# The end of a sixteen-head attention: its last twenty units over six PSUM banks, and a split output projection

## The reference

```python
keys    = xn @ triu(Wk).T        # xn: layer-normalised x
queries = xn @ tril(Wq).T
values  = xn @ Wv.T              # each reshaped to (b, t, 16, 8)
att = softmax(queries . keys * scale)
x = x + (att . values).reshape(b, t, 128) @ Wu.T + bu
```

## Time and profile before

| | |
|---|---|
| median of 3 runs | 1685.22 us (1685.16 to 1686.24) |
| the profiled execution's own time | 1684.64 us |
| its span | 1682.9 us |
| mean granted clock of TensorE | 0.951 of full speed |
| PE busy | 1525.1 us (91%) |
| DVE busy | 1378.1 us (82%) |
| ACT busy | 921.6 us (55%) |
| POOL busy | 300.4 us (18%) |

### The profile page before, as it was taken

How to read it: one execution, slowest core, us unless ns; L and a number is a source line. 1 busy time by engine, 2 the same in 40 slices (tenths; PEclk the granted TensorE clock), 3 DMA queues, 4 the chain that set the end, 5 groups by cost and what they waited for, 6 DMA issues and landing times. The chain is left out here.

```text
span 1682.9 us, 24089 instructions
## 1 busy us (share of the span) xinstructions
PE 1525.1 (91%) x8530; PEld 759.5 (45%) x8530; DVE 1378.1 (82%) x2435; ACT 921.6 (55%) x1751; POOL 300.4 (18%) x366
## 2 busy tenths in 40 slices
PE   6899999999999999869998888876999969989698
PEld 2111111111111111158884333332788758869587
DVE  6999999999999997357673999999766657887686
ACT  3088888888888888823334666663422232222232
POOL 3200000000000000000012888785000110020000
PEclk7599999999999999979999999999999988999799
DMA  3340011000000000200000212221000002200123
GB/s 96 108 146 24 26 30 31 28 24 23 23 23 24 24 24 5 51 9 1 1 1 24 78 65 68 70 67 34 1 1 1 1 1 97 80 28 1 51 75 104
DMA packets 41233, 66.07 MB, mean 39 GB/s; under 512 B 11422, under 2 KB 18511, under 8 KB 40392
## 3 DMA queue, kind: packets, MB, share of 16 engines
q1 hardware_dynamic: 41112, 64.52, 12.7%
HBM read 56.72 MB, written 6.88 MB: 38 GB/s over the span
## 5 line engine op out<-in xcount | busy, mean ns | idle before, releaser
L785 DVE TENSOR_REDUCE row_max<-ps 128x1 f32<-128x1024 f32 x512 | 601.0, 1219 | 34.3 <-PE ps L590 18.1
L708 ACT ACTIVATE probs<-ps 128x512 f32<-128x512 f32 x1024 | 529.0, 604 | 127.6 <-PE ps L605 127.3
L605 PE MATMUL ps<-q_stack,k_stack 51*128 51x512 bf16 x1024 | 346.9, 387 | 8.7 <-ACT probs L708 6.7
L590 PE MATMUL ps<-k_stack,q_stack 48*128 48x512 bf16 x1024 | 325.9, 404 | 20.3 <-DVE row_max L785 10.6
L622 PE MATMUL ps<-probs,v_head 128*16 128x512 f32 x2048 | 270.0, 600 | 0.0
L590 PEld LDWEIGHTS ps<-k_stack,q_stack 48*128 48x128 bf16 x1024 | 58.7, 96 | 368.3 <-DVE row_max L785 342.0
L1298 PE MATMUL ps<-s_hc,ident 128*128 128x512 f32 x256 | 139.0, 628 | 47.8 <-DVE s_hc L1571 42.8
L951 ACT ACTIVATE x_gate<-ps 128x512 f32<-128x512 f32 x128 | 76.3, 598 | 183.8 <-PE ps L122 183.6
L1223 POOL TENSOR_TENSOR s_dbx<-s_dx,s_b_rows 128x512 f32<-128x512 f32 x128 | 159.4, 1270 | 35.1 <-DVE s_h L1562 34.6
L1562 DVE TENSOR_TENSOR_SCAN s_h<-ps,s_state,s_dbx 128x512 f32<-128x512 f32 x128 | 156.7, 1264 | 4.6 <-POOL s_dbx L1223 2.8
L605 PEld LDWEIGHTS ps<-q_stack,k_stack 51*128 51x128 bf16 x1024 | 76.1, 94 | 131.7 <-ACT probs L708 128.1
(11 more groups left out here) (339 smaller groups left out, 1866.9 us busy)
## 6 DMA issues: line engine op xcount, KB each, us to landing
s_b_rows<-s_b_dram SPq DMA_DIRECT2D x64, 256.0 KB, 3.1
y_spread<-y_probs_dram SPq DMA_DIRECT2D x128, 128.0 KB, 3.0
q_stack<-q_parts_dram SPq DMA_DIRECT2D x30, 96.0 KB
k_stack<-k_parts_dram SPq DMA_DIRECT2D x30, 96.0 KB
w_w<-w_dram SPq DMA_DIRECT2D x1, 2048.0 KB, 8.0
o_dram<-o_sb SPq DMA_DIRECT2D x64, 32.0 KB
q_stack<-q_parts_dram SPq DMA_DIRECT2D x30, 64.0 KB
k_stack<-k_parts_dram SPq DMA_DIRECT2D x30, 64.0 KB
```

The source lines that it names most:

```text
L590: last = nc.tensor.matmul(core.ps[:, 2 * b + r, :], qst[buf][0:KROWS, u * P:(u + 1) * P], kst[buf][0:KROWS, key:key + CH], start=True, sto ...
L605: nc.tensor.matmul(core.ps[:, S_BANK + n % S_RING, :], kst[buf][HALF:ROWS, kt * P:(kt + 1) * P], qst[buf][HALF:ROWS, c * CH:(c + 1) * CH], ...
L708: nc.scalar.activation(probs[:, us % RING, c * CH:(c + 1) * CH], core.ps[:, S_BANK + n % S_RING, :], ACT.Exp).then_inc(exp_done, 1)
L785: nc.vector.tensor_reduce(mx[:, u, b:b + 1], core.ps[:, 2 * b:2 * b + 2, :], mybir.AxisListType.XY, ALU.max).then_inc(max_done, 1)
```

## The change

- **Twenty units by themselves.** The units 236 to 255 (`TAIL` to `UNITS`), whose scores came in `slot` after the last maxima, get a loop of their own. Scores go in turn to the six banks 6, 4, 5, 0, 1, 2 and wait for the exp six places back; the first three still for the one three back; the fourth and the sixth also for the last maxima. Odd scores read rows 0 to 50 of the stacks, even ones rows 64 to 114. For that the ones and maxima of heads 14 and 15 are also placed in rows 48 to 50, by four added DMAs (two of ones at the start, one behind each head's maxima).
- **Heads 0 to 13** are loaded before head 15's maxima are stored in SP's list, and divided as before. **Head 14** goes the way that head 15 went (`late`), into rows 112 to 119 of `attT`.
- **Projection of heads 0 to 14** (rows 0 to 119 of `attT`): four groups of four matmuls, behind the values of the units 251 to 254, all into bank 3. DVE adds each to `x`, and the next group waits for that.
- **Head 15** isn't stored. PE takes `o_sb` itself as the weight, rows 32c to 32c+15, against `Wu_last`, a new weight array of 129 columns: 8 rows of Wu's last head, a ninth whose last column is 1, which brings the denominator, and zeros. The sixteen matmuls write three tiles to bank c and the fourth to bank 4+c. DVE takes the reciprocals of the denominators (two instructions per chunk) and adds each tile times its reciprocal to `x` (16 `scalar_tensor_tensor`). The next norm's statistics come after the second chunk instead of the first.
- Filling `attT` and `den` with ones at the start is dropped.

The core of the diff:

```diff
+    UNITS = HEADS * NT
+    TAIL = UNITS - LAG_S
+    TAIL_BANKS, EARLY_OUT_BANK, LAST_TILES = (6, 4, 5, 0, 1, 2), 3, 3
+    OUT_UNITS = range(UNITS - NC_ - 1, UNITS - 1)
...
@@ sync
                 sp.dma_start(qst[par][HALF + KROWS:ROWS, :], md[par]).then_inc(m_loaded[par], 16)
+                if head >= HEADS - 2:
+                    sp.dma_start(qst[par][KROWS:KROWS + NPART, :], md[par]).then_inc(low_loaded[head % 2], 16)
...
+            for head in (HEADS - 2, HEADS - 1):
+                sp.dma_start(kst[head % NBUF][KROWS:KROWS + NPART, :], ones[:]).then_inc(low_ones_placed, 16)
...
             store_o(HEADS - 3)
+            sp.wait_ge(o_stored, O_STORE * (HEADS - 2))
+            for which, dst in enumerate((attT, den)):
+                sp.dma_start(dst[0:MOST, :], od[which, 0:HEADS - 2]).then_inc(fin_loaded, 16)
             store_max(HEADS - 1, (HEADS - 1) % NBUF)
             store_o(HEADS - 2)
-
             sp.wait_ge(o_stored, O_STORE * (HEADS - 1))
-            sp.wait_ge(cleared, 2)
-            for which, dst in enumerate((attT, den)):
-                sp.dma_start(dst[0:FULL, :], od[which, 0:HEADS - 1]).then_inc(fin_loaded, 16)
-            store_o(HEADS - 1)
-            sp.wait_ge(o_stored, O_STORE * HEADS)
             for which in range(2):
                 sp.dma_start(late[:, which, :],
-                             od[which, HEADS - 1].rearrange("s (k n) -> (s k) n", n=P)).then_inc(late_loaded, 16)
-            sp.wait_ge(att_ready, NC_)
+                             od[which, HEADS - 2].rearrange("s (k n) -> (s k) n", n=P)).then_inc(late_loaded, 16)
             sp.wait_ge(late_ready, 1)
-            sp.dma_start(attT[FULL:P, :].rearrange("s (k n) -> s k n", n=P), late[:, 0, :]).then_inc(late_placed, 16)
+            sp.dma_start(attT[MOST:FULL, :].rearrange("s (k n) -> s k n", n=P), late[:, 0, :]).then_inc(late_placed, 16)
@@ tensor
+            def tail_score(n):
+                m, c = TAIL + n // NC_, n % NC_
+                head, kt = m // NT, m % NT
+                buf = head % NBUF
+                if n == 0 or kt == 0 and c == 0:
+                    pe.wait_ge(m_loaded[buf], 16 * (m // BODY + 1))
+                    pe.wait_ge(low_loaded[head % 2], 16)
+                if n in (3, 5):
+                    pe.wait_ge(max_done, 2 * UNITS - 1 + n // 5)
+                if n < S_RING:
+                    pe.wait_ge(exp_done, 4 * TAIL + n - S_RING + 1)
+                elif n >= len(TAIL_BANKS):
+                    pe.wait_ge(exp_done, 4 * TAIL + n - len(TAIL_BANKS) + 1)
+                rows = slice(0, KROWS + NPART) if n % 2 else slice(HALF, ROWS)
+                nc.tensor.matmul(core.ps[:, TAIL_BANKS[n % len(TAIL_BANKS)], :], kst[buf][rows, kt * P:(kt + 1) * P],
+                                 qst[buf][rows, c * CH:(c + 1) * CH], start=True, stop=True).then_inc(s_done, 1)
+
+            def project_out(g):
+                if g == 0:
+                    core.loaded(pe, "Wu0", "Wu_last")
+                    pe.wait_ge(att_ready, NC_)
+                    pe.wait_ge(late_placed, 16)
+                    pe.wait_ge(max_done, 2 * UNITS)
+                else:
+                    pe.wait_ge(out_added, g)
+                for k in range(TPC):
+                    last = nc.tensor.matmul(core.ps[:, EARLY_OUT_BANK, k * P:(k + 1) * P],
+                                            attT[0:FULL, (g * TPC + k) * P:(g * TPC + k + 1) * P], w["Wu0"][0:FULL, :],
+                                            start=True, stop=True)
+                last.then_inc(out_done, 1)
...
-            for gs in range(NT + LAG_V):
-                slot(LOOPED, gs, gs < NT, gs < NT + LAG_S)
-
-            core.loaded(pe, "Wu0")
-            pe.wait_ge(att_ready, NC_)
-            pe.wait_ge(late_placed, 16)
-            for g in range(NC_):
+            for gs in range(NT):
+                slot(LOOPED, gs)
+            pe.wait_ge(low_ones_placed, 32)
+            for m in range(TAIL, UNITS):
+                for c in range(NC_):
+                    tail_score(NC_ * (m - TAIL) + c)
+                weigh_values(m - 2)
+                if m in OUT_UNITS:
+                    project_out(m - OUT_UNITS.start)
+            weigh_values(UNITS - 2)
+            weigh_values(UNITS - 1)
+
+            pe.wait_ge(evacuated, HEADS)
+            pe.wait_ge(out_added, NC_)
+            for c in range(NC_):
                 for k in range(TPC):
-                    last = nc.tensor.matmul(core.ps[:, g, k * P:(k + 1) * P], tile_of(attT, g * TPC + k), w["Wu0"][:],
-                                            start=True, stop=True)
-                last.then_inc(out_done, 1)
+                    bank, col = (c, k * (P + 1)) if k < LAST_TILES else (NC_ + c, 0)
+                    last = nc.tensor.matmul(core.ps[:, bank, col:col + P + 1],
+                                            o_sb[32 * c:32 * c + VROWS, k * P:(k + 1) * P],
+                                            w["Wu_last"][32 * c:32 * c + VROWS, :], start=True, stop=True)
+                last.then_inc(last_done, 1)
@@ scalar
+            for m in range(TAIL, UNITS):
+                if m % NT == 2:
+                    evacuate(m // NT - 1)
+                act.wait_ge(pv_done, m - (RING - 1))
+                for c in range(NC_):
+                    n = NC_ * (m - TAIL) + c
+                    act.wait_ge(s_done, 4 * TAIL + n + 1)
+                    nc.scalar.activation(probs[:, m % RING, c * CH:(c + 1) * CH],
+                                         core.ps[:, TAIL_BANKS[n % len(TAIL_BANKS)], :], ACT.Exp).then_inc(exp_done, 1)
@@ vector
+                nc.vector.tensor_tensor(xs, xs, core.ps[:, EARLY_OUT_BANK, :].rearrange("p (k d) -> p k d", d=P),
+                                        ALU.add).then_inc(out_added, 1)
+            for c in range(NC_):
+                dve.wait_ge(last_done, c + 1)
+                t = c * TPC
+                outs = core.ps[:, c, 0:LAST_TILES * (P + 1)].rearrange("p (k n) -> p k n", n=P + 1)
+                nc.vector.reciprocal(last_rden[:, t:t + LAST_TILES], outs[:, :, P]).then_inc(last_rden_ready, 1)
+                nc.vector.reciprocal(last_rden[:, t + LAST_TILES:t + TPC],
+                                     core.ps[:, NC_ + c, P:P + 1]).then_inc(last_rden_ready, 1)
+                dve.wait_ge(last_rden_ready, 2 * (c + 1))
+                if c == 0:
+                    dve.wait_ge(out_added, NC_)
+                for k in range(TPC):
+                    part = outs[:, k, 0:P] if k < LAST_TILES else core.ps[:, NC_ + c, 0:P]
+                    line.mark(nc.vector.scalar_tensor_tensor(out=core.x[:, t + k, :], in0=part,
+                                                             scalar=last_rden[:, t + k:t + k + 1],
+                                                             in1=core.x[:, t + k, :], op0=ALU.mult, op1=ALU.add))
+                if c == 1:
                     line.wait(dve)
                     following.stat_rows(dve, 0)
```

More of the change, by code:

```diff
@@ L302, in softmax_attention @@
         late = sb("late", [P, 2, P])
-        FULL = (HEADS - 1) * HD
+        MOST, FULL = (HEADS - 2) * HD, (HEADS - 1) * HD
+        last_rden = sb("last_rden", [P, NT])
         qd = nc.dram_tensor("q_parts_dram", (HEADS, NPART, HD, T), BF16).ap()
@@ L346, in softmax_attention @@
         fin_loaded = core.sem("a_fin_loaded")
-        cleared = core.sem("a_cleared")
+        low_ones_placed = core.sem("a_low_ones_placed")
+        low_loaded = [core.sem(f"a_low_loaded{i}") for i in range(2)]
         late_loaded = core.sem("a_late_loaded")
@@ L354, in softmax_attention @@
         out_done = core.sem("a_out_done")
+        out_added = core.sem("a_out_added")
+        last_done = core.sem("a_last_done")
+        last_rden_ready = core.sem("a_last_rden_ready")
         bias_added = core.sem("a_bias_added")
@@ L507, in _ @@
                 stage_v(head, head)
-            for a in (attT, den):
-                nc.gpsimd.memset(a[:], 1.0).then_inc(cleared, 1)
             core.loaded(pool, "bu")
@@ L568, in _, with weigh_values @@
             core.loaded(pe, "Wv0")
+            def weigh_values(m):
+                buf, kt = m // NT % NBUF, m % NT
+                if kt == 0:
+                    pe.wait_ge(v_staged, m // NT + 1)
+                    if m:
+                        pe.wait_ge(evacuated, m // NT)
+                pe.wait_ge(exp_done, 4 * m + 4)
+                for c in range(NC_):
+                    last = nc.tensor.matmul(core.ps[32 * c:32 * c + VROWS, O_BANK, :], v_head[buf][:, kt, :],
+                                            probs[:, m % RING, c * CH:(c + 1) * CH],
+                                            start=kt == 0, stop=kt == NT - 1)
+                last.then_inc(pv_done, 1)
@@ L613, in slot @@
                 if values:
[L614 to L625, removed]
+                    weigh_values(j * BODY + gs - LAG_V)
             for gs in range(BODY):
@@ L725, in _ @@
```

(26 more changed lines are left out.)

## The result

| | before | after |
|---|---|---|
| median | 1685.73 us (4 runs, 1685.16 to 1687.53) | 1668.30 us (4 runs, 1667.05 to 1668.85) |
| profiled execution: time, span | 1684.64, 1682.9 | 1668.66, 1666.9 |

The ratio is 0.9894, 95% interval 0.9877 to 0.9911: faster, by 17.4 us or 1.1%. Forecast were 1669.5 and a range of 1666 to 1674.

A forecast was written before the change was run, and what follows sets the result against it. DVE's maxima pace the attention; the last twenty units were bound by a loop through PE, the end by one chain. Tail -7.5, exit -9.4 and clock +1.2 gave -15.7, so 1669.5 us, range 1666 to 1674.

The forecast's parts named there:

- Tail: Last twenty units to the last values' end: six banks let ACT pace, -9.1 us; -7.5 us together with the added projections.
- Projections: Four groups for the other heads amid the last units, 1.1 us of PE each, 2.63 per unit: +2.2 us.
- Inputs: Loads and placed rows for the last units arrive in time: cost 0, or 0.5 us if head 15's load lands late.
- Head 14's margin: Time between head 14's placing and the first projection's need of it, at unit 251: 6.3 us.
- Rival D: Early projection's inputs late, stopping PE in unit 251; beyond 6.3 us each microsecond costs one, 5 would give 1674.5; chance 0.05.
- Rival B: Paired scores in the last units don't run side by side; 2.4 us more, 1672; chance 0.08.
- Rival C: ACT doesn't keep 0.485 with more banks, or the loop closes elsewhere; only the exit gains, 1677; chance 0.05.
- rival E: PE's clock falls in the last twenty units because it is less busy there; 1694; chance 0.03.
- Exit: From the last values to the norm rows' end: 10.1 us against 19.55, DVE pacing at 1.39 per chunk; -9.4 us.
- Clock: PE stands about 5 us while DVE finishes, so the next stage runs longer at half clock; +1.2 us, bounds 0 and 2.8.

The follow-up runs named there:

- one half: The changed kernel with all scores of the tail read from rows 64 to 114, so none can run beside another; 1669.05 us.
- The profile with the clock held: The changed kernel with 28 added matmuls of zeros on PE behind the last head's projection; 1669.23 us over six runs.
- the banks alone: The kernel before with the tail's scores on six banks, all from rows 64 to 114, and its old end; 1677.70 us, ratio 0.9954.
- fillers: 28 matmuls of zeros added on PE behind the last head's projection, in two variants of the changed kernel; 1669.23 and 1668.46 us.
- the projections behind: The changed kernel with the projection of heads 0 to 14 behind the last values instead of amid units 251 to 254; 1672.48 us.
- both spread ones: Two profiles of the changed kernel with projections behind units 248, 250, 252 and 254 instead of 251 to 254; 1666.68 and 1666.74 us.
- second profile with fillers: The changed kernel with projections behind units 248, 250, 252 and 254 and 28 added matmuls of zeros behind the last head's projection; 1668.46 us.

## Why the prediction was right

- **Tail.** Predicted -7.5, measured -7.2. The loop through PE that explained 2.44 was the cause: three banks bring it back, six alone take 8.7 off. ACT's pitch is 0.490 and not 0.485, 0.4 us over 80.
- **Projections.** Predicted +2.2, measured +2.04 (41.83 - 39.79), with 2.61 per unit where 2.63 was predicted. The description of the change puts the projections behind the values of the units 251 to 254; they stand in the turns of these units, behind the values of 249 to 252, as the prediction's own sum has it. The Trainium skill, TensorEngine Tiling (Array Packing), section Tiling Modes, says that a change of tiling mode drains the engine; whatever that costs here is inside the 1.09 that a group took.
- **Inputs.** Head 15's load made PE wait 0.59 at unit 240 and cost nothing, as the sum said. Yet the prediction named a PE wait for DMA at unit 240 as a sign of being wrong; by its own times (scores from 670.2, load landed by 671.1) it should have expected one, so this sign came true without meaning anything. Head 14's margin was 5.4 us instead of 6.3: its two loads took 3.65 us from issue to DVE (680.02 to 683.67) where head 15's had taken 2.25. Rival D's rule, one for one beyond the margin, is too mild: 2.4 us more were lost to the clock.
- **Rival B** has a premise that came true: in the plain units the scores are freed one by one (1.05 for four instead of 0.53), and that costs nothing, since ACT paces. In the units with projections the four go in 0.53, so B's cost didn't occur; all scores from one half would cost 1.9 us of tail there. **Rival C** and **rival E** fall too: 24 exps without a gap, and a granted clock of 1.00 from 663 to 706.
- **Exit.** Predicted -9.4, measured -9.8: a DVE chunk is 1.31 instead of 1.39, and the old end took 19.2 behind six banks too, the new one 9.74 behind three. PE was faster than thought, 2.82 us for sixteen matmuls instead of about 4, which changes nothing since DVE paces.
- **Clock.** Predicted +1.2. The stretch that was meant shows it: the next stage's four transposes take 1.08 us instead of 0.63 and the eight records behind them (w_gate) 1.88 instead of 1.06, all at half the clock, so that from the norm rows' end to the first dense matmul it is 4.46 instead of 3.22, +1.24, and 4.45 in the other two profiles of the changed kernel. The profile with the clock held has 3.22 again. But three things keep this from being the confirmation that the numbers suggest. First, were misread: the clock was not still 0.50 at 738 to 740. It had come back, and fell anew as the experts began:

```profile
732.00:734.00 2.00, 0.00 (x0) 0.00 (x0) 1.64 (x6) 0.00 (x0) 0.09 (x1) 1.00 0.00 0
734.00:736.00 2.00, 0.71 (x5) 0.50 (x5) 0.92 (x4) 1.72 (x4) 0.01 (x1) 1.00 0.01 4
736.00:738.00 2.00, 2.00 (x12) 1.77 (x13) 1.19 (x2) 1.87 (x3) 0.00 (x0) 0.79 0.00 0
```

Second, the start of the experts loses clock with the old end as well: with the banks alone the same distance was 3.76, and 952.6 us lay behind the norm rows. Third, over all runs the medians are 1686.05 (32 runs of the kernel before) and 1667.97 (12 of the changed one), 18.1 apart, where tail and exit give 17.0. So in the medians nothing was given back, as far as this estimate goes, and the 1.7 of the first pair of profiles isn't shown to be the change's: the same code behind the norm rows took 946.7 to 952.6 us in the profiles without fillers. That the term's size was met is in part luck; without it the forecast would have been 1668.3.

## What to carry to other kernels

When an engine has short regular gaps, add up the loop that ends in them: here a wait (0.65 us), a turn to the values (0.32), the values (0.98) and a score's latency (0.49) made exactly one unit of 2.44, and the number of buffers, not an engine, was the term to change. Work that fills another engine's slack costs only what exceeds the pace, so it belongs where the slack is, but not before its inputs have landed. In the chain of DMAs at this stage's end the links took 4.4, 2.3 and 3.2 us; an operand that PE can read where it lies, with the normalisation put behind the product, removed them all. And when two profiles agree with a forecast to 0.1 us in a stretch that scatters by more, look at further profiles.

## What was not expected of the hardware

- A projection with 16 rows of weight in the array and 129 columns took 2.82 / 16 = 0.18 us at a granted clock of 1.00, against 1.95 / 8 = 0.24 for 128 rows and 128 columns.
- The clock can fall while PE works. In the profiles of the projections behind, of one half, of both spread ones and of the second of the changed kernel it fell to 0.50 while these sixteen small matmuls ran; they took 3.01 to 4.88 us instead of 2.82. DVE paced all the same, except that with the projections behind, where it fell earliest, DVE's first step came 0.6 us later. In the second profile with fillers it fell at 710.6, although PE had been idle for only 0.2 us since them; in the first profile of the changed kernel, without fillers, it had fallen at 710.8. In the first the same fillers kept 1.00. So the pause alone isn't the cause of the fall, and continuous issue didn't prevent it; what decides it isn't settled here.
- Between profiles of the same code behind the norm rows the time varies by up to 6 us, more than most of the edits tried; the timeline of the stretch was needed to size them.
